# Cross-attention and feed-forward block: early rows of maxima split, transposed and sent ahead of norms, constants and key transfers

## The chip, the core and the metric

One core of one Trainium2 chip runs the kernel. The metric is the device time of one execution in microseconds; the median of several runs is given, with their lowest and highest. Some times below come from one execution that the hardware profiler recorded.

## The reference, cut to what matters

```python
def layer(x, ctx, pos):                 # x (4,256,256), ctx (4,256,128), float32
    h = layernorm(x)
    q = rope(h @ Wq)                    # 32 heads of 8
    k, v = rope((ctx @ Wkv)[k half]), (ctx @ Wkv)[v half]
    w = softmax(q k^T / sqrt(8))        # over 256 keys
    x = x + (w @ v) @ Wout + bout
    h = layernorm(x)
    up = square(relu(h @ up_w)) @ down_w            # 256 -> 1024 -> 256
    moe = (h @ expert_weight) * sum(top2(h @ gate_w))
    return x + layernorm(up + moe) * gamma + beta
```

## The kernel before

The work is cut into 8 tiles of 128 tokens (two for each of 4 batches). Attention is done in 32 rows, numbered M: four rows for each tile of queries, and a row holds 8 heads. Each row goes through these steps:

- **Scores once, for the maxima.** Four units `S(M, i)` of matmuls of queries by keys, each into one PSUM bank of 128x512. VectorE reduces each unit to its negated maxima (`rd.M.i`, line 744, the tile mneg), and so frees the bank.
- **Split.** GpSimd splits the maxima into a high and a low part (`mh.M`, lines 536 and 537, the tile mnat).
- **Transpose.** TensorE transposes them (`MT.M`, the helper at line 817), ScalarE copies the result to mT (`aMT.M`, line 556), and SyncE sends it by DMA into spare rows of qstack (`sM.M`, line 465). Thus the second product has the maximum subtracted in it.
- **Scores again, transposed.** Four units `ST(M, i)` (line 856); ScalarE takes the exponential (`ex.M.i`, line 627). `PV.M` (line 940) multiplies by the values, and the rest is the output projection and the feed-forward part.

A burst `B.a.b@banks` issues two units ST (for a over 0) and two units S (for b over 0) together. Beside that stand, for each batch b, `cT.b` and `K.b` (context and keys), `xT.b` and `Q.b` (normed tokens transposed, query product), VectorE's `dK` and `dQ` (two products each by cosine and sine, lines 732 and 733), the turn by `pad` (lines 350 and 351, on GpSimd for most), `hi` and `lo` (the halves of the value, ScalarE line 615, VectorE or GpSimd line 358), and `sc`, the DMAs that put these into kstack and qstack (line 377). `nm1.b` is the norm of a batch (line 409), and `stackq.i` a memset of a qstack (line 491).

The order of the work is written out by hand in five tables, one for each engine: PE_ORDER, DVE_ORDER, ACT_ORDER, POOL_ORDER and SP_ORDER. Each engine runs its table strictly in order and waits by semaphores. The digits behind @ in PE_ORDER name the PSUM banks of the units. A unit that takes a bank waits until the unit that had it before is emptied, by the engine that reads it. With 8 banks, this ties the order of one engine to that of the others: an entry waits at the head of its engine's table, and all that stands behind it waits too.

Transposes are matmuls with the identity; a float32 matmul appears twice in the trace. Row M may be sent only while the mT buffer M mod 2 is free, and mneg has 3 buffers.

Of the kernel before, what the change touches and what calls it, by code (L numbers as in the profile page):

```python
# [5 lines left out]

PE_ORDER = """
id.7 cT.0@0 id.8 TR.0@1 K.0@2 id.2 xT.0.0@3 id.14 xT.0.1@4 Q.0.0@5 Q.0.1@6 V.0@0 cT.1@1 TR.1@3 id.4 K.1@2 V.1@4
TR.2@5 TR.3@6 cT.2@0 id.23 B.0.1@13 B.0.2@72 xT.1.0@1 B.0.3@42 B.0.4@67 B.0.5@13 B.0.6@54 Q.1.0@0 MT.0@6
B.0.7@12 B.0.8@76 xT.2.0@5 MT.1@4 K.2@2 B.1.9@6541 Q.2.0@0 B.2.10@5617 B.3.0@43 xT.3.0@5 MT.2@0 B.0.11@16 PV.0@0  # L10
MT.3@7 B.4.12@6307 Q.3.0@5 MT.4@2 B.5.13@4160 PV.1@3 B.6.14@7254 B.7.15@0136 MT.5@5 B.8.16@2405 MT.6@3 PV.2@1
B.9.17@7524 PV.3@0 B.10.18@6137 B.11.19@4520 o.0@1 MT.7@7 PV.4@6 B.12.20@2534 B.13.21@0671 MT.8@2 aT.0@3 PV.5@5
B.14.22@4310 B.15.23@2756 W.0@4 MT.9@1 MT.10@3 B.16.24@0267 PV.6@4 B.17.25@1350 B.18.26@6274 PV.7@1 B.19.27@0256
# [14 lines left out]
"""  # L28
DVE_ORDER = """
ang bn1.0.0 bn1.0.1 nm1.0.0 dK.k.0 nm1.0.1 pad.k.0 lo.k.0 dQ.q.0.0 dQ.q.0.1 bn1.1.0 bn1.2.0 lo.q.0.0 dK.k.1  # L30
bn1.3.0 lo.q.0.1 pad.k.1 rd.0.2 rd.0.1 rd.0.0 rd.0.3 rd.1.2 rd.1.0 rd.2.2 rd.1.3 rd.1.1 rd.2.0 rd.2.1 rd.3.3
# [987 lines left out]
```

How the kernel before makes its waits and increments, by code:

```python
        def filled(eng, e):  # L310
            eng.wait_ge(bg_full, FULL[e])
# [4 lines left out]
        def taken(eng, e):  # L317
            eng.wait_ge(bank_free[BANK[e]], TURN[e] + 1)
# [15 lines left out]
        def sent_before(eng, w, b):  # L335
            if b >= 1 and w == "k":
                eng.wait_ge(k_sent[b - 1], 96)
            elif b >= 1:
                for p in range(len(tokens_of(b - 1))):
                    eng.wait_ge(q_sent[b - 1, p], 96)
# [1 line left out]
        def turn_pairs(eng, e):  # L343
            w, b, n = e[1], e[2], cols(e)
            taken(eng, ("K", b) if w == "k" else ("Q", b, e[3]))
            for before in jobs_before(e):
                eng.wait_ge(lo_ready[before], 1)
            r, c, d = rotated[w], by_cos[w], by_sin[w]
            ins = eng.tensor_tensor(r[:, 0, n], c[:, 0, n], d[:, 1, n], ALU.subtract)
            ins = eng.tensor_tensor(r[:, 1, n], c[:, 1, n], d[:, 0, n], ALU.add)
            ins.then_inc(rotated_ready[job(e)], 1)
# [1 line left out]
        def low_part(eng, e):  # L354
            w, b, n = e[1], e[2], cols(e)
            eng.wait_ge(hi_ready[job(e)], 1)
            sent_before(eng, w, b)
            eng.tensor_tensor(lo[w][:, :, n], rotated[w][:, :, n], hi[w][:, :, n].bitcast(f32), ALU.subtract)\
                .then_inc(lo_ready[job(e)], 1)
# [1 line left out]
        def to_stack(eng, e, waited):  # L361
# [8 lines left out]
            if (e[1:-1], high) not in waited:  # L370
                waited.add((e[1:-1], high))
                eng.wait_ge((hi_ready if high else lo_ready)[job(e[:-1])], 1)
                eng.wait_ge(const[at], 1)
```

## Time and profile before

| | us |
|---|---|
| median of 3 runs | 213.78 |
| lowest and highest | 211.82, 215.93 |
| profiled execution | 210.77 |
| its span in the trace | 209.0 |
| TensorE busy in the span | 190.0 |
| VectorE, ScalarE, GpSimd busy | 142.8, 120.5, 84.5 |

The span runs from the first to the last instruction of the trace, the time of the profiled execution includes 1.77 us around it. Busy time counts pipelined matmuls as the profile models their ends, so a busy TensorE need not be at its peak. A row of the timeline gives its start, its length, the engine and line, what it writes and reads with the count, and in brackets how long the engine had been idle before and who released it.

### The profile page before, as it was taken

What the parts mean: (1) busy time and instruction counts of PE and PEld (TensorE: products, weight loads), DVE (VectorE), ACT (ScalarE), POOL (GpSimd) and SP (SyncE); (2) the same over time, 40 slices, a digit from 0 to 9 for tenths busy, and PEclk for the clock granted to TensorE, in tenths of its full rate; (3) what the DMA queues carried; (4) which work ended last, traced back from release to release, by engine and by line L of the source; (5) the groups of instructions that cost most, each with busy time, mean ns of one, the idle gap of its engine ahead of it and who ended that gap; (6) DMA issues with size and microseconds to landing.
All of it is one profiled execution on the core that took longest, in us unless ns stands there. A gap on an engine that the chain in (4) does not pass through costs nothing.

```text
span 209.0 us, 6609 instructions
## 1 busy us (share of the span) xinstructions
PE 190.0 (91%) x2506; PEld 161.0 (77%) x2506; DVE 142.8 (68%) x297; ACT 120.5 (58%) x275; POOL 84.5 (40%) x169
## 2 busy tenths in 40 slices
PE   3989498878899999999999999999999999999990
PEld 2889376656777878888777888778999988999980
DVE  1689497998899888678899986775420558245324
ACT  5743433579788987858676777769572111421400
POOL 6549787982933202410472314121211116263203
PEclk9999958999999999999999999999999999999997
DMA  6919632486544300000042000000000000000001
GB/s 165 313 30 271 130 85 47 107 241 181 168 129 106 108 9 6 3 3 3 5 125 62 5 3 8 5 3 28 5 3 0 28 22 31 0 2 3 25 0 50
DMA packets 15999, 13.15 MB, mean 63 GB/s; under 512 B 2912, under 2 KB 15584, under 8 KB 15968
## 3 DMA queue, kind: packets, MB, share of 16 engines
q1 hardware_dynamic: 11136, 9.32, 15.9%
q10 hardware_dynamic: 4832, 3.42, 6.4%
q8 instruction: 20, 0.33, 0.7%
q14 instruction: 11, 0.09, 0.1%
HBM read 5.13 MB, written 1.05 MB: 30 GB/s over the span
## 4 chain that ended last, share of the span: by engine, by line
PE 66%; DMA 10%; SPq 6%; DVE 4%; issue 4%; POOL 3%; ACT 3%; ACTq 1%; POOLq 0%; DVEq 0%
PE ps L823 24%; PE ps L991 12%; PE ps L940 10%; PE ps L856 9%; PE ps L817 6%; PE ps L846 4%; DMA qstack<-mT 3%; SPq L377 3%; DMA x_sb<-in_x 3%; DMA qstack<-hi_q 2%; ACT probs L627 2%; DMA kstack<-lo_k 1%; SPq L437 1%; ACTq L377 1%; DVE xn L409 1%
## 5 line engine op out<-in xcount | busy, mean ns | idle before, releaser
L744 DVE TENSOR_REDUCE mneg<-ps 128x2 f32<-128x512 f32 x128 | 81.0, 683 | 15.2 <-PE ps L846 15.0
L627 ACT ACTIVATE probs<-ps 128x512 f32<-128x512 f32 x128 | 69.1, 595 | 15.3 <-PE ps L856 13.9
L856 PEld LDWEIGHTS ps<-qstack,kstack 32*128 32x128 f32 x512 | 32.7, 185 | 14.6 <-issue 10.3
L856 PE MATMUL ps<-qstack,kstack 32*128 32x128 f32 x512 | 40.0, 282 | 3.2 <-DMA qstack<-mT 1.5
L940 PE MATMUL ps<-probs,vaug 128*32 128x128 f32 x1024 | 34.0, 275 | 0.6 <-ACT probs L627 0.4
L846 PE MATMUL ps<-kstack,qstack 32*128 32x256 f32 x256 | 32.0, 338 | 2.5 <-DMA qstack<-hi_q 2.1
L823 PE MATMUL ps<-x2nT,up 128*128 128x128 f32 x256 | 31.0, 276 | 0.1
L823 PEld LDWEIGHTS ps<-x2nT,up 128*128 128x128 f32 x256 | 30.2, 192 | 0.7 <-issue 0.2
L991 PE MATMUL ps<-down,inner 128*128 128x256 f32 x128 | 29.5, 379 | 0.0
L940 PEld LDWEIGHTS ps<-probs,vaug 128*32 128x32 f32 x1024 | 26.3, 109 | 3.5 <-issue 1.6
L536 POOL TENSOR_SCALAR mnat<-mneg 128x8 fp32r<-128x8 f32 x32 | 7.6, 236 | 49.2 <-DVE mneg L744 37.8
L991 PEld LDWEIGHTS ps<-down,inner 128*128 128x128 f32 x128 | 23.5, 190 | 2.9 <-issue 0.2
L846 PEld LDWEIGHTS ps<-kstack,qstack 32*128 32x128 f32 x256 | 19.3, 190 | 4.3 <-issue 3.3
L660 ACT ACTIVATE whole<-ps 128x512 f32<-128x512 f32 x16 | 9.6, 602 | 18.0 <-PE ps L823 17.8
L503 POOL TENSOR_SCALAR var_eps<-mv 128x1 f32<-128x1 f32 (+1 forms) x21 | 5.3, 251 | 36.0 <-DVE mv L674 35.8
L548 POOL TENSOR_TENSOR inner<-whole 128x512 f32<-128x512 f32 x9 | 9.4, 1045 | 18.0 <-ACT whole L660 18.0
L504 POOL TENSOR_TENSOR rstd<-var_eps,neg_half 128x1 f32<-128x1 f32 (+1 forms) x21 | 12.9, 613 | 1.7
L788 DVE TENSOR_TENSOR y<-ps,moe 128x256 f32<-128x256 f32 x8 | 3.4, 422 | 14.5 <-PE ps L991 14.5
L556 ACT ACTIVATE oT<-ps 128x128 f32<-128x128 f32 x32 | 8.9, 279 | 6.6 <-PE ps L940 6.3
L883 PE MATMUL ps<-ident 128*128 128x128 f32 x58 | 9.0, 312 | 3.4 <-POOL ident L488 3.4
L556 ACT ACTIVATE mT<-ps 16x128 fp32r<-16x128 f32 x32 | 8.1, 258 | 6.7 <-PE ps L817 5.3
L883 PEld LDWEIGHTS ps<-ident 128*128 128x128 f32 x58 | 7.9, 163 | 3.5 <-POOL ident L488 3.4
(95 smaller groups left out, 251.9 us busy)
## 6 DMA issues: line engine op xcount, KB each, us to landing
kstack<-hi_k SPq DMA_DIRECT2D x12, 128.0 KB, 2.6
qstack<-hi_q SPq DMA_DIRECT2D x11, 128.0 KB, 3.1
kstack<-lo_k SPq DMA_DIRECT2D x8, 128.0 KB, 2.5
result<-x_sb SPq DMA_DIRECT2D x8, 128.0 KB, 1.7
down<-in_L_ffn_down_w ACTq DMA_DIRECT2D x3, 256.0 KB, 4.1
qstack<-lo_q SPq DMA_DIRECT2D x5, 128.0 KB, 2.6
x_sb<-in_x SPq DMA_DIRECT2D x2, 256.0 KB, 5.1
up<-in_L_ffn_up_w SPq DMA_DIRECT2D x1, 512.0 KB, 6.6
```

Source lines behind the costliest of these rows:

```text
L504: pool.tensor_tensor(rstd[:, i, a:z], var_eps[:, i, a:z], neg_half[:, 0:z - a], ALU.pow)\
L556: emptied(act.activation(to, of, ACT.Copy), e)
L627: act.activation(probs[M % NPROBS][:, i, :, :, :], bg(("ST", M, i))[:].rearrange("p (s t n) -> p s t n", s=2, t=T), ACT.Exp, scale=SCALE). ...
L660: emptied(act.activation(whole[j][:], bg((f"up{j}", u))[:].rearrange("p (f n) -> p f n", f=4), ACT.Relu), (f"up{j}", u))
L744: emptied(dve.tensor_reduce(mneg[M % NNEG][:, i, :], bg(("S", M, i))[:].rearrange("p (s k) -> p s k", s=2), AX.X, ALU.max, negate=True), ( ...
L817: ins = pe.transpose(bg(e)[0:rows, at:at + P], block_, ident[:])
L823: ins = pe.matmul(to, lhs[k], rhs[k], start=(k == 0), stop=(k == len(lhs) - 1))
L846: return pe.matmul(bg(("S", M, i))[:, s * N:(s + 1) * N], qstack[b][strip(i), 2 * m + s, tile(t)], kstack[b % 2][strip(i), 2 * m + s, :], ...
L856: return pe.matmul(bg(("ST", M, i))[:, at:at + P], kstack[b % 2][strip(i), 2 * m + s, tile(k)], qstack[b][strip(i), 2 * m + s, tile(t)], s ...
L883: pe.transpose(ps[WARM][:, 0:P], ident[:], ident[:])
L940: ins = pe.matmul(bg(e)[strip(i), 0:P], vaug[b % 2][:, k, NM * i + m, 2 * HD * s:2 * HD * s + Q], probs[M % NPROBS][:, i, s, k, :], start= ...
L991: ins = pe.matmul(bg(("dn", u))[:, 0:D], inner[u % 2][:, f, :], down[:, f, :], start=(f == 0), stop=(f == FT - 1))
```

## The change

The tables alone are edited; the instructions and the banks of each entry stay the same. In PE_ORDER MT.0 goes ahead of B.0.6 and Q.1.0, MT.1 ahead of xT.2.0, MT.2 and B.2.10 ahead of Q.2.0, and K.2 behind B.3.0. DVE_ORDER has the reductions of rows 1 to 4 in another order. ACT_ORDER has aMT.0 ahead of the key DMAs, aMT.1 ahead of axT.2.0, aMT.2 ahead of ex.0.3 and hi.q.1.0. POOL_ORDER has mh.0 ahead of nm1.2.0, and the memsets stackq.2 and stackq.3 behind mh.3 and mh.4. SP_ORDER has sM.0 ahead of the key transfers and sM.2 ahead of the query transfers of batch 1.

```diff
 PE_ORDER = """
...
-TR.2@5 TR.3@6 cT.2@0 id.23 B.0.1@13 B.0.2@72 xT.1.0@1 B.0.3@42 B.0.4@67 B.0.5@13 B.0.6@54 Q.1.0@0 MT.0@6
-B.0.7@12 B.0.8@76 xT.2.0@5 MT.1@4 K.2@2 B.1.9@6541 Q.2.0@0 B.2.10@5617 B.3.0@43 xT.3.0@5 MT.2@0 B.0.11@16 PV.0@0
+TR.2@5 TR.3@6 cT.2@0 id.23 B.0.1@13 B.0.2@72 xT.1.0@1 B.0.3@42 B.0.4@67 B.0.5@13 MT.0@6 B.0.6@54 Q.1.0@0
+B.0.7@12 B.0.8@76 MT.1@4 xT.2.0@5 B.1.9@6541 B.2.10@5617 MT.2@0 Q.2.0@0 B.3.0@43 K.2@2 xT.3.0@5 B.0.11@16 PV.0@0
...
 DVE_ORDER = """
...
-bn1.3.0 lo.q.0.1 pad.k.1 rd.0.2 rd.0.1 rd.0.0 rd.0.3 rd.1.2 rd.1.0 rd.2.2 rd.1.3 rd.1.1 rd.2.0 rd.2.1 rd.3.3
-rd.3.1 rd.3.2 dQ.q.1.0 rd.4.3 rd.3.0 rd.4.2 rd.2.3 dQ.q.2.0 rd.4.0 lo.q.1.0 rd.4.1 rd.5.3 dK.k.2 rd.5.2 rd.5.0
+bn1.3.0 lo.q.0.1 pad.k.1 rd.0.2 rd.0.1 rd.0.0 rd.0.3 rd.1.0 rd.1.2 rd.2.2 rd.1.3 rd.1.1 rd.2.1 rd.2.0 rd.3.1
+rd.3.2 rd.2.3 dQ.q.1.0 rd.3.3 rd.4.3 rd.3.0 rd.4.2 dQ.q.2.0 rd.4.0 lo.q.1.0 rd.4.1 rd.5.3 dK.k.2 rd.5.2 rd.5.0
...
 POOL_ORDER = """
...
-rs1.3.0 nm1.2.0 mh.0 stackq.2 mh.1 lo.k.1 nm1.3.0 pad.q.1.0 stackq.3 mh.2 mh.3 pad.q.2.0 mh.4 pad.k.2 mh.5
+rs1.3.0 mh.0 nm1.2.0 mh.1 lo.k.1 nm1.3.0 mh.2 pad.q.1.0 mh.3 stackq.2 mh.4 stackq.3 pad.q.2.0 pad.k.2 mh.5
...
```

On TensorE, around the query product of batch 2, this stood before (L856 are units ST, L846 units S, L817 transposes, L823 products; mnat are the maxima, Q.b reads xnT and wq_rows, K.b reads cT and wk_rows):

```order
L823 MATMUL ps<-cT,wk_rows 128x256 x2
L856 MATMUL ps<-qstack,kstack 128x128 x2
L846 MATMUL ps<-kstack,qstack 128x256 x2
L856 MATMUL ps<-qstack,kstack 128x128 x4
L846 MATMUL ps<-kstack,qstack 128x256 x2
L856 MATMUL ps<-qstack,kstack 128x128 x2
L823 MATMUL ps<-xnT,wq_rows 128x256 x4
```

The same place now:

```order
L846 MATMUL ps<-kstack,qstack 128x256 x2
L856 MATMUL ps<-qstack,kstack 128x128 x4
L846 MATMUL ps<-kstack,qstack 128x256 x2
L856 MATMUL ps<-qstack,kstack 128x128 x4
L846 MATMUL ps<-kstack,qstack 128x256 x2
L856 MATMUL ps<-qstack,kstack 128x128 x2
L817 MATMUL ps<-ident,mnat 16x128
L823 MATMUL ps<-xnT,wq_rows 128x256 x4
L856 MATMUL ps<-qstack,kstack 128x128 x8
L823 MATMUL ps<-cT,wk_rows 128x256 x2
```

Between the bursts B.1.9 and B.2.10 no product stands any more: the query product (Q.2.0) has moved behind the second burst and behind the transpose of the maxima of row 2, and the key product behind B.3.0.

On ScalarE, the same stretch before (mT0 and mT1 are the two buffers of transposed maxima, probs the exponentials, ps0 is PSUM bank 0):

```order
L556 ACTIVATE mT0<-ps6 16x128
L556 ACTIVATE xnT<-ps5 128x512
L556 ACTIVATE mT1<-ps4 16x128
L627 ACTIVATE probs0<-ps5 128x512
L627 ACTIVATE probs0<-ps6 128x512
L615 ACTIVATE hi_q<-rotated_q 128x512
L627 ACTIVATE probs0<-ps5 128x512
```

and now:

```order
L556 ACTIVATE mT0<-ps6 16x128
L377 DMA kstack1<-hi_k 16x8x256 x2
L556 ACTIVATE mT1<-ps4 16x128
L556 ACTIVATE xnT<-ps5 128x512
L627 ACTIVATE probs0<-ps5 128x512
L627 ACTIVATE probs0<-ps6 128x512
L627 ACTIVATE probs0<-ps5 128x512
L556 ACTIVATE mT0<-ps0 16x128
```

The copy of row 2's maxima out of bank 0 (the last row) now stands behind the third exponential and ahead of the fourth; before, it stood behind the fourth and the query work.

On GpSimd, before (mnat is the split of the maxima, the MEMSETs fill qstack2 and qstack3):

```order
L350 TENSOR_TENSOR rotated_q<-by_cos_q,by_sin_q 128x256
L351 TENSOR_TENSOR rotated_q<-by_cos_q,by_sin_q 128x256
L491 MEMSET qstack3 128x2048
L536 TENSOR_SCALAR mnat0<-mneg2 128x4x2
L537 TENSOR_TENSOR mnat0<-mneg2,mnat0 128x4x2
L536 TENSOR_SCALAR mnat1<-mneg0 128x4x2
L537 TENSOR_TENSOR mnat1<-mneg0,mnat1 128x4x2
```

and now:

```order
L491 MEMSET qstack2 128x2048
L536 TENSOR_SCALAR mnat0<-mneg1 128x4x2
L537 TENSOR_TENSOR mnat0<-mneg1,mnat0 128x4x2
L491 MEMSET qstack3 128x2048
L350 TENSOR_TENSOR rotated_q<-by_cos_q,by_sin_q 128x256
L351 TENSOR_TENSOR rotated_q<-by_cos_q,by_sin_q 128x256
L350 TENSOR_TENSOR rotated_k<-by_cos_k,by_sin_k 128x256
```

Both memsets come later: qstack3's now stands behind the split of row 4 and ahead of the query turn of batch 2 and the key turn.

## Rows read from the trace of the kernel before

**Rows 1.** The page: busy time, share and instructions by engine

```profile
PE 190.0 (91%) x2506; PEld 161.0 (77%) x2506; DVE 142.8 (68%) x297; ACT 120.5 (58%) x275; POOL 84.5 (40%) x169
```

**Rows 2.** Stretches: length, busy PE, PEld, DVE, ACT, POOL (count), clock, DMA share, GB/s

```profile
20.00:35.00 15.00, 11.99 (x74) 9.09 (x72) 10.21 (x21) 5.25 (x12) 11.48 (x15) 0.77 0.44 101
35.00:50.00 15.00, 12.37 (x174) 9.25 (x172) 14.00 (x24) 9.89 (x23) 11.11 (x18) 1.00 0.58 158
50.00:65.00 15.00, 13.27 (x280) 10.59 (x283) 13.99 (x25) 12.91 (x33) 8.30 (x16) 1.00 0.55 157
65.00:100.00 35.00, 34.19 (x656) 28.42 (x645) 28.36 (x51) 28.94 (x69) 7.82 (x26) 1.00 0.11 28
...
22.14:25.57 3.43, 0.52 (x8) 0.34 (x8) 0.79 (x2) 2.16 (x5) 2.73 (x4) 1.00 0.51 117
25.57:32.40 6.83, 6.75 (x28) 5.08 (x29) 5.97 (x10) 1.88 (x4) 5.27 (x8) 0.50 0.33 77
35.50:40.00 4.50, 3.56 (x42) 2.85 (x41) 4.50 (x9) 2.57 (x5) 4.50 (x5) 1.00 0.23 62
```

**Rows 3.** TensorE's timeline from 24 to 49 us

```profile
24.27 0.52 PE L846 MATMUL ps<-kstack,qstack 32*128 32x256 f32 x8 [2.13 <-DMA qstack<-hi_q]
...
29.02 3.65 PE L823 MATMUL ps<-xnT,wq_rows 128*128 128x256 f32 x8
...
32.70 1.02 PE L846 MATMUL ps<-kstack,qstack 32*128 32x256 f32 x8
...
35.25 0.33 PE L856 MATMUL ps<-qstack,kstack 32*128 32x128 f32 x2
...
36.50 1.97 PE L823 MATMUL ps<-xnT,wq_rows 128*128 128x256 f32 x8 [0.57 <-DVE by_sin_q L733]
38.40 0.33 PE L856 MATMUL ps<-qstack,kstack 32*128 32x128 f32 x2
...
40.57 0.28 PE L817 MATMUL ps<-ident,mnat 128*16 128x128 f32 x1
...
48.30 0.33 PE L856 MATMUL ps<-qstack,kstack 32*128 32x128 f32 x2
```

**Rows 4.** VectorE's timeline from 27 to 39 us

```profile
27.46 4.28 DVE L744 TENSOR_REDUCE mneg<-ps 128x2 f32<-128x512 f32 x7 [0.20 <-PE ps L846]
33.27 1.89 DVE L744 TENSOR_REDUCE mneg<-ps 128x2 f32<-128x512 f32 x3 [1.53 <-PE ps L846]
...
38.67 0.68 DVE L732 TENSOR_TENSOR by_cos_q<-ps,table 128x512 f32<-128x512 f32 x1
```

**Rows 5.** The chain that ended last: start, us, what

```profile
40.31 0.22 POOL mnat L537
...
47.94 4.65 DMA qstack<-mT
...
59.20 2.47 DMA qstack<-mT
```

**Rows 6.** GpSimd's timeline from 26 to 44 us

```profile
26.88 2.44 POOL L409 TENSOR_SCALAR xn<-x_sb,mv,rstd 128x256 f32<-128x256 f32 x2 [1.93 <-PE ps L817]
...
38.25 1.81 POOL L491 MEMSET qstack<- 128x2048 f32 x1
40.03 0.20 POOL L536 TENSOR_SCALAR mnat<-mneg 128x8 fp32r<-128x8 f32 x1
...
43.62 0.72 POOL L350 TENSOR_TENSOR rotated_k<-by_cos_k,by_sin_k 128x256 f32<-128x256 f32 x1 [0.30 <-DVE by_sin_k L733]
```

**Rows 7.** ScalarE's timeline from 39 to 47 us

```profile
39.09 0.60 ACT L627 ACTIVATE probs<-ps 128x512 f32<-128x512 f32 x1
...
45.06 0.63 ACT L615 ACTIVATE hi_k<-rotated_k 128x512 fp32r<-128x512 f32 x1
46.59 0.27 ACT L556 ACTIVATE mT<-ps 16x128 fp32r<-16x128 f32 x1 [0.90 <-DMA qstack<-mT]
```

**Rows 8.** TensorE's waits from 46 to 112 us: total, times, longest

```profile
PE ps L856 <- DMA qstack<-mT: 1.5, 3, 0.9
```

More of the change, by code:

```diff
@@ L48 @@
 sc.k.0.0 aV.0 acT.1 aTR.1 hi.q.0.0 ldup.1 sc.q.0.0.0 sc.q.0.0.3 sc.q.0.0.2 hi.q.0.1 sc.q.0.0.1 sc.q.0.1.0
-sc.q.0.1.3 exptab aV.1 aTR.3 axT.1.0 aTR.2 hi.k.1 acT.2 sc.k.1.1 sc.k.1.3 aMT.0 axT.2.0 aMT.1 ex.0.1 ex.0.0
-hi.q.1.0 ex.0.2 sc.q.1.0.3 ex.0.3 lddown.0 aMT.2 sc.q.1.0.5 ex.1.1 aPV.0 aMT.3 axT.3.0 ex.1.0 ex.1.2 ex.1.3
+sc.q.0.1.3 exptab aV.1 aTR.3 axT.1.0 aTR.2 hi.k.1 acT.2 aMT.0 sc.k.1.1 sc.k.1.3 aMT.1 axT.2.0 ex.0.1 ex.0.0
+ex.0.2 aMT.2 ex.0.3 hi.q.1.0 sc.q.1.0.3 lddown.0 sc.q.1.0.5 ex.1.1 aPV.0 aMT.3 axT.3.0 ex.1.0 ex.1.2 ex.1.3
 lddown.2 ldvec.0 hi.k.2 aMT.4 ex.2.0 ex.2.1 aPV.1 hi.q.2.0 ex.2.3 ex.3.0 aMT.5 ex.3.1 ex.2.2 ex.3.2 ex.3.3
@@ L77 @@
 ldwkv ldx.0.0 ldx.2.0 ldx.1.0 ldx.0.1 ldc.2 ldup.0 ldc.1 sc.k.0.2 sc.k.0.3 sc.k.0.5 ldvec.1 sc.k.0.4 sc.q.0.0.4
-sc.q.0.0.5 sc.q.0.1.2 sc.q.0.1.1 sc.q.0.1.5 sc.q.0.1.4 sc.k.1.2 sc.k.1.0 sM.0 ldexpert.1 sc.k.1.4 sM.1 sc.k.1.5
-sc.q.1.0.1 sc.q.1.0.2 sc.q.1.0.0 sM.2 ldexpert.0 sc.q.1.0.4 sM.3 ldwout ldc.3 sM.4 lddown.1 sc.q.2.0.1
+sc.q.0.0.5 sc.q.0.1.2 sc.q.0.1.1 sc.q.0.1.5 sc.q.0.1.4 sM.0 sc.k.1.2 sc.k.1.0 sM.1 ldexpert.1 sc.k.1.4 sc.k.1.5
+sM.2 sc.q.1.0.1 sc.q.1.0.2 sc.q.1.0.0 ldexpert.0 sc.q.1.0.4 sM.3 ldwout ldc.3 sM.4 lddown.1 sc.q.2.0.1
 sc.q.2.0.3 sM.5 sc.q.2.0.0 sc.q.2.0.5 sc.q.2.0.2 sc.q.2.0.4 sM.6 sc.q.3.0.1 sc.q.3.0.3 sM.7 sc.q.3.0.0
```

## The prediction

> **What bounds the kernel now.** I read the totals first: TensorE is busy 190.0 of 209.0 us [rows 1], so the end moves only if TensorE's idle time or its clock moves. The stages say where that can be [rows 2]. From 65 to 100 us TensorE is busy 34.19 of 35 us and VectorE only 28.36: what arrives late at 65 us stays late. Between 35 and 65 us it is VectorE that is full (14.00 and 13.99 of 15) while TensorE has 2.63 and 1.73 us idle. From 20 to 35 us both wait, and the granted clock averages 0.77. The change lies in the last two of these, so I followed 24 to 50 us engine by engine.
>
> I use the names of the order tables. B.0.3 is a burst of matmuls, MT.M the transpose of the maxima of row M, Q.b the query product of batch b, rd a reduction by VectorE, dQ its two products, ex an exponential.
>
> TensorE [rows 3]: two bursts at 24.27, then Q.1.0 from 29.02 for 3.65 us at half clock (the same product took 1.97 us at full clock, Q.2.0 at 36.50). Only behind it stand MT.0 and B.0.7, B.0.8 (32.70). B.1.9, the first burst that uses maxima, starts at 35.25, and B.2.10 at 38.40. MT.2 comes at 40.57. VectorE [rows 4] does seven reductions in 4.28 us, so one each (4.28 - 0.68)/6 = 0.60 us; it waits 1.53 us for the burst behind Q.1.0, starts again at 33.27, and takes Q.2.0's result at 38.67. The chain of waits [rows 5] runs over a memset of GpSimd (38.25 in [rows 6]), the maxima at 40.31, and a transfer of maxima sent at 47.94 that took 4.65 us behind larger ones (another took 2.47).
>
> **Part 1: MT.0 goes ahead of B.0.6 and Q.1.0.** rd.0.3 ends at 27.26. GpSimd, which now does the split before the norm, takes about 0.5 us for the two steps (row 2's began at 40.03 [rows 6] and ended at 40.31 + 0.22 = 40.53 [rows 5]), so maxima are ready at 27.8. MT.0 also needs bank 6, so rd.1.0, which now stands before rd.1.2. It can begin when B.0.4 is full, some 0.15 us after the 27.46 at which the reductions went on before: 27.61 to 28.29. MT.0 runs at 28.3, and the copy by ScalarE behind cT's ends near 29.05. SyncE sends it at 29.1, where before MT.0 itself had to wait for the end of Q.1.0 at 32.5. Past it go two key transfers on either queue, about 0.65 us later each; keys of batch 1 are not read before batch 1's first burst, beyond 50 us, so that costs nothing. rd.1.2, which B.0.6 waits for, is one reduction (0.60) and those 0.15 us later, so B.0.6 and Q.1.0 behind it are 0.75 late: Q.1.0 starts at 29.77, with the clock back near 32.4, and B.0.7 and B.0.8 run together at 32.93, the latter no longer waiting for mT. VectorE now asks first for a bank of B.0.8 (rd.3.1), which is full at 33.45. It restarts at 33.50, before 33.27. So this part, which sends maxima 4 us earlier, leaves VectorE 0.23 us later. The norm of batch 2 moves from 26.88 to 27.8, takes 2.44 us [rows 6] and ends at 30.2, well before its transposes at 33.5: hidden.
>
> **Part 2: rd.2.3 ahead, MT.2 ahead of Q.2.0.** VectorE: rd.3.1 at 33.50, rd.3.2, rd.2.3, dQ.1.0 (35.30 to 36.50: two instructions of 0.68 us as the reductions, so 0.60 apart, 1.20), rd.3.3, rd.4.3, rd.3.0 (37.70 to 38.38), rd.4.2 to 38.98. B.1.9 needs rd.3.2 alone and starts at 34.9, 0.35 earlier. B.2.10 needs rd.3.0, so 38.50, 0.1 later. Before, Q.2.0 filled the time between these two bursts (36.50 to 38.40) and VectorE took its result at once, at 38.67. Now Q.2.0 stands behind MT.2, in the same bank 0, and behind B.2.10. So it must wait for B.2.10 (38.5), MT.2 (39.0), and the copy aMT.2, which on ScalarE stands behind ex.0.2, an exponential of B.2.10 that took 0.60 us and began 0.69 after it (39.09 in [rows 7]): 39.2 to 39.8, copy to 40.0. Q.2.0 starts at 40.05, needs 1.97 us at full clock and is there at 42.02. VectorE's next instruction after rd.4.2 is dQ.2.0: **it waits from 38.98 to 42.07**, against 38.67 before: +3.4 us on the engine that is full in this stage. The gain on the other side: mT.2 leaves at 40.0, earlier than before, where MT.2 was only transposed at 40.57, and ahead of the large query transfers; the 0.90 us that ScalarE waited for it at 46.59 [rows 7] goes.
>
> **Part 3: two memsets of GpSimd go behind the splits.** Each takes 1.81 us [rows 6]. They no longer delay MT.2. But the split of row 4 must wait for rd.4.1, now at 45.14 (dQ.2.0 43.26, rd.4.0, lo, rd.4.1), and behind it stand a memset (1.8), the query turn (1.4) and the key turn (0.72 twice): 45.65 + 1.8 + 1.4 + 1.45 = 50.3. In before the key turn started at 43.62. ScalarE has hi_k next in its order, at 45.06 before [rows 7], now at 50.35, and behind it the copy of MT.4 (51.1) and ex.2.0 (done 51.7). B.6.14 needs both: 51.75 instead of 48.30 [rows 3], +3.45 us. That is the lag leaving the changed region at full clock.
>
> **The clock.** In before the granted clock was 1.00 until 25.57, though TensorE had been busy only 0.52 of the 3.43 us ahead of it, and was 0.50 for the next 6.83 us, in which it was busy 6.75 [rows 2]. The new order makes such a stretch again: B.1.9 ends near 35.6, then nothing until 38.5, then B.2.10 (0.6) and MT.2 (0.3), nothing until 40.05. That is 0.9 busy of 4.5 us, where before had 3.56 of 4.5 and kept 1.00 [rows 2]. I expect a second fall near 39 us. All of Q.2.0 would then run at half: 3.65 - 1.97 = 1.7 more, so the bounds of this term are 0 and 1.7, and something more if K.2 and PV.0 run slow too, which VectorE's five instructions after Q.2.0 (3 us) partly hide. I take 1.7, since the earlier low stretch lasted 6.8 us although TensorE was full.
>
> The Trainium skill ("TensorE: Matmul & The Clock Gate", Part 4: PE-mode transpose) states that transposes do not count as busy for the clock in the way matmuls do. By that rule MT.2 would hold nothing up and the fall would be surer; the sum would be the same. No row here separates the two kinds. On transfers "DMA: Bandwidth & Descriptors" (Queues, rings and completion order) says that a transfer's completion write lands only after every earlier write of that DMA engine. By that rule sending small maxima ahead of large transfers gives back up to 4.65 - 2.47 = 2.2 us per transfer; the trace agrees that they differ so, and the saving would speak for the change (the third case below).
>
> **What comes back.** TensorE's waits after 46 us for transfers of maxima are 1.5 us in three [rows 8], of which 0.86 lies before B.6.14 and is counted already; 0.6 is left, which a late kernel hides. The idle of VectorE (1.01) and TensorE (1.73) between 50 and 65 us bounds what the stretch can take back. With a small lag I take 1.2, with a large one 1.7.
>
> **The sum.** Against the profiled execution (210.77 us, span 209.0): 3.45 + 1.7 - 1.7 = +3.4, so 214.2. The three runs have a median of 213.78, 3.0 above it; the difference carries over: 217.2.
>
> **Rivals.**
> 1. The replay holds but the clock doesn't fall again: 3.45 - 1.2 = +2.2, 216.0. For it: a burst of 0.6 us lies in the middle of the gap. Against: [rows 2], the fall at 25.57. Chance 0.2.
> 2. Faster: maxima are the bound, as the chain [rows 5] says. Then MT.2 at 39.0 instead of 40.57 gives 1.5, and the waits for transfers 0.6 more: -2.1, 211.7. It decides if VectorE's wait for Q.2.0 is made up by the work that piles up behind it before 65 us. Against: VectorE has only 1.0 us idle in 15. Chance 0.15.
> 3. The order has slack that cancels, the stall is shorter than computed, say 0.6 us: no change, 213.8. Chance 0.12.
> 4. No catching up, and K.2, xT.3.0 and PV.0 slow as well: 3.45 + 1.7 + 0.5 = +5.6, 219.4. Chance 0.1.
>
> The main case has the remaining 0.43. A measurement of this kernel can tell about 2% from no change, here 4.28 us. Slower by more than that: rival 4 and a quarter to a third of the main case, 0.24. Faster by more than 2%: a third of rival 2, 0.05. Within: 0.71. The range reaches from near rival 2, 212.5, to beyond rival 4, 220.5.
>
> **What would show it.** Right: B.0.7 near 32.9 and VectorE going on at 33.5; no matmul between about 35.6 and 38.5; Q.2.0 starting near 40.05 behind a copy of mT; a gap of VectorE before by_cos_q of 3 to 5 us; a granted clock of 0.5 from about 39; the key turn past 50 us; more idle of TensorE in the stage from 35 to 50, and an unchanged stage after 80 us. Wrong: Q.2.0 before 39, a VectorE gap under 1 us there, or a TensorE that is back on the old times by 65 us.

## Result and profile after

The changed kernel takes 219.55 us (median of 4 runs, 218.26 to 220.34), the kernel before 213.53 us (median of its 4): slower, ratio 1.030 with a 95% interval of 1.021 to 1.039. The profiled execution took 218.26 us, span 216.5 against 209.0.

Each run also reports the mean clock that TensorE was granted, and this number matters here: the same kernel runs at different clocks from run to run. In seven of the twelve profiled executions of the experiments (e2, e3, e4, e6, e7, e9, e11) it was at least 0.01 below the kernel's median; from those I read waits, their causes and the course of the clock, never a total. Ratios compare only runs that were not disturbed (within 1.5% of their kernel's fastest), each with the runs of before made beside it, while medians are over all runs.

The page of the changed kernel: span, busy time by engine, TensorE's busy tenths and the granted clock in 40 slices.

```profile
span 216.5 us, 6609 instructions
...
PE 194.3 (90%) x2506; PEld 164.2 (76%) x2506; DVE 142.2 (66%) x297; ACT 120.5 (56%) x275; POOL 84.0 (39%) x169
...
PE   3999395699888999999999999999999999999990
...
PEclk9999958558999999999999999999999999999997
```

TensorE is busy 4.3 us longer for the same 2506 matmuls, and the clock row has a second low stretch two slices after the first. The stages, to be read beside [rows 2]:

```profile
20.00:35.00 15.00, 10.62 (x67) 7.81 (x65) 9.11 (x18) 5.30 (x12) 9.25 (x13) 0.77 0.41 93
35.00:50.00 15.00, 11.03 (x65) 8.16 (x69) 8.09 (x14) 3.66 (x8) 7.92 (x12) 0.55 0.40 108
50.00:65.00 15.00, 12.82 (x252) 9.93 (x245) 13.16 (x23) 11.94 (x28) 10.54 (x17) 1.00 0.55 143
65.00:100.00 35.00, 33.42 (x611) 27.44 (x603) 29.47 (x55) 29.20 (x71) 9.26 (x28) 1.00 0.20 54
33.08:36.49 3.41, 2.12 (x27) 1.31 (x25) 2.46 (x5) 1.25 (x3) 1.77 (x2) 1.00 0.06 7
36.49:50.14 13.65, 10.51 (x57) 7.78 (x61) 6.74 (x13) 3.03 (x7) 6.57 (x11) 0.50 0.42 118
```

From 35 to 50 us VectorE is busy 8.09 us instead of 14.00, and the clock is 0.55 instead of 1.00. Where VectorE was full, it now waits. The last two lines show the clock's fall: in the 3.41 us before it TensorE was busy 2.12, and in the low stretch it was busy 10.51 of 13.65 us. In before, the stretch behind the first low stretch looked like this, and no fall followed:

```profile
32.40:35.82 3.42, 3.40 (x31) 2.35 (x29) 2.55 (x5) 1.01 (x3) 2.25 (x3) 1.00 0.11 18
```

TensorE's timeline, for [rows 3]:

```profile
24.40 0.51 PE L846 MATMUL ps<-kstack,qstack 32*128 32x256 f32 x8 [2.62 <-DMA qstack<-hi_q]
...
29.89 3.55 PE L823 MATMUL ps<-xnT,wq_rows 128*128 128x256 f32 x8
33.37 0.52 PE L846 MATMUL ps<-kstack,qstack 32*128 32x256 f32 x8
...
35.37 0.33 PE L856 MATMUL ps<-qstack,kstack 32*128 32x128 f32 x2 [0.83 <-DVE mneg L744]
...
39.05 0.47 PE L856 MATMUL ps<-qstack,kstack 32*128 32x128 f32 x2 [3.02 <-DVE mneg L744]
...
41.05 3.75 PE L823 MATMUL ps<-xnT,wq_rows 128*128 128x256 f32 x8 [0.58 <-ACT mT L556]
...
45.78 2.07 PE L823 MATMUL ps<-cT,wk_rows 128*128 128x256 f32 x4
...
49.36 1.43 PE L940 MATMUL ps<-probs,vaug 128*32 128x128 f32 x32
...
55.74 0.33 PE L856 MATMUL ps<-qstack,kstack 32*128 32x128 f32 x2
```

Q.1.0 starts at 29.89 and B.0.7 at 33.37. B.1.9 runs at 35.37, then B.2.10 comes after 3.02 us of idle. Q.2.0 starts at 41.05 (36.50 before) and takes 3.75 us, K.2 (45.78) takes 2.07 where it took 1.03, and PV.0 starts at 49.36 where it started at 41.36. B.6.14 starts at 55.74, 7.4 us late. VectorE, for [rows 4]:

```profile
27.73 4.27 DVE L744 TENSOR_REDUCE mneg<-ps 128x2 f32<-128x512 f32 x7 [0.35 <-PE ps L846]
34.03 1.89 DVE L744 TENSOR_REDUCE mneg<-ps 128x2 f32<-128x512 f32 x3 [2.02 <-PE ps L846]
...
44.84 0.69 DVE L732 TENSOR_TENSOR by_cos_q<-ps,table 128x512 f32<-128x512 f32 x1 [5.34 <-PE ps L823]
...
49.50 0.69 DVE L744 TENSOR_REDUCE mneg<-ps 128x2 f32<-128x512 f32 x1 [1.57 <-PE ps L846]
```

The wait ahead of by_cos_q is 5.34 us, against none in before. There is another of 1.57 us at 49.50, for B.0.11 behind the slow K.2 and xT.3.0. GpSimd and ScalarE, for [rows 6, 7]:

```profile
39.42 1.81 POOL L491 MEMSET qstack<- 128x2048 f32 x1
48.02 0.20 POOL L536 TENSOR_SCALAR mnat<-mneg 128x8 fp32r<-128x8 f32 x1 [6.80 <-DVE mneg L744]
...
48.45 1.81 POOL L491 MEMSET qstack<- 128x2048 f32 x1
...
51.59 0.72 POOL L350 TENSOR_TENSOR rotated_k<-by_cos_k,by_sin_k 128x256 f32<-128x256 f32 x1
```

```profile
53.21 0.63 ACT L615 ACTIVATE hi_k<-rotated_k 128x512 fp32r<-128x512 f32 x1
```

Row 4's split waits 6.80 us, then come the memset, the query turn and the key turn (51.59), and hi_k is at 53.21 instead of 45.06.

The lateness is then carried to the end almost without change. PV.3, PV.4 and PV.6 begin 8.0, 7.8 and 8.0 us later than in before, a PV row near 97 us 8.0, and the last PV row, at 173.8 us in before, 7.5. The span is 7.5 longer.

### The profile page after: what moved, and what is told of

Its sections match the earlier page's. It is cut to its first block, busy times and chain, and to the rows that moved or that the text cites. A ratio compares the mean times of both kernels' runs of the same rounds, so it can differ in the third digit from the quotient of the medians.

```text
span 216.5 us, 6609 instructions
## 1 busy us (share of the span) xinstructions
PE 194.3 (90%) x2506; PEld 164.2 (76%) x2506; DVE 142.2 (66%) x297; ACT 120.5 (56%) x275; POOL 84.0 (39%) x169
## 3 DMA queue, kind: packets, MB, share of 16 engines
q10 hardware_dynamic: 4832, 3.42, 6.0%
HBM read 5.13 MB, written 1.05 MB: 29 GB/s over the span
## 4 chain that ended last, share of the span: by engine, by line
PE 71%; DVE 9%; DMA 5%; issue 5%; ACT 3%; POOL 2%; SPq 2%; ACTq 1%; POOLq 0%; DVEq 0%
PE ps L823 28%; PE ps L991 12%; PE ps L940 10%; PE ps L856 10%; PE ps L817 6%; DVE mneg L744 5%; PE ps L846 4%; DMA qstack<-hi_q 2%; DMA qstack<-lo_q 2%; PE ps L883 2%; SPq L377 2%; ACT probs L627 1%; DMA qstack<-mT 1%; ACTq L377 1%; POOL qstack L491 1%
## 5 line engine op out<-in xcount | busy, mean ns | idle before, releaser
L856 PEld LDWEIGHTS ps<-qstack,kstack 32*128 32x128 f32 x512 | 33.5, 189 | 19.3 <-issue 13.1
L856 PE MATMUL ps<-qstack,kstack 32*128 32x128 f32 x512 | 41.1, 286 | 7.4 <-DVE mneg L744 4.1
L846 PE MATMUL ps<-kstack,qstack 32*128 32x256 f32 x256 | 32.4, 342 | 2.8 <-DMA qstack<-hi_q 2.6
L823 PE MATMUL ps<-x2nT,up 128*128 128x128 f32 x256 | 31.0, 276 | 0.0
L823 PEld LDWEIGHTS ps<-x2nT,up 128*128 128x128 f32 x256 | 30.2, 192 | 0.7
L536 POOL TENSOR_SCALAR mnat<-mneg 128x8 fp32r<-128x8 f32 x32 | 7.1, 221 | 59.3 <-DVE mneg L744 47.9
L846 PEld LDWEIGHTS ps<-kstack,qstack 32*128 32x128 f32 x256 | 19.8, 194 | 4.4 <-issue 4.3
L823 PE MATMUL ps<-xnT,wq_rows 128*128 128x256 f32 (+1 forms) x40 | 11.2, 443 | 0.6 <-ACT mT L556 0.6
```

The source lines that it names most:

```text
L823: ins = pe.matmul(to, lhs[k], rhs[k], start=(k == 0), stop=(k == len(lhs) - 1))
L846: return pe.matmul(bg(("S", M, i))[:, s * N:(s + 1) * N], qstack[b][strip(i), 2 * m + s, tile(t)], kstack[b % 2][strip(i), 2 * m + s, :], ...
L856: return pe.matmul(bg(("ST", M, i))[:, at:at + P], kstack[b % 2][strip(i), 2 * m + s, tile(k)], qstack[b][strip(i), 2 * m + s, tile(t)], s ...
```

## Experiments

Clocks differ between runs, so I give for each kernel its median, the ratio with its interval, the median of the runs' mean clocks, and the span reduced to full clock: over the 54 runs of before the span grows by 0.39 us for each microsecond spent at half clock (2 x (1 - clock) x span), and that much is taken off each run's span. The reduced span in the table is the mean over a kernel's runs. These scatter by 0.4 to 1.5 us (standard deviation), so that a mean over 4 runs is good to 0.2 to 0.8 us; and the reduction is rough where another kernel's low stretches lie in other places. For the changed kernel it runs from 207.5 to 210.7.

| kernel | median us | ratio to before, 95% | median clock | reduced span |
|---|---|---|---|---|
| before (54 runs) | 214.05 | 1 | 0.959 | 205.6 |
| changed | 219.55 | 1.030 (1.021 to 1.039) | 0.948 | 209.0 |
| e1 changed, idle matmuls in the gap | 218.79 | 1.013 (0.992 to 1.034) | 0.958 | 209.3 |
| e2 changed, Q.2.0 ahead again | 216.17 | 1.012 (0.997 to 1.028) | 0.968 | 208.7 |
| e3 changed, Q.2.0 ahead of MT.2 | 222.08 | 1.031 (1.016 to 1.046) | 0.942 | 210.0 |
| e4 before, 41 warming transposes | 212.25 | 0.996 (0.990 to 1.001) | 0.972 | 206.6 |
| e5 before with part 1 alone | 214.94 | 1.012 (0.977 to 1.047) | 0.952 | 205.8 |
| e6 before, Q.2.0 behind B.2.10 | 213.90 | 1.013 (0.995 to 1.031) | 0.963 | 206.3 |
| e7 as e1, memset moved | 216.00 | 1.015 (0.984 to 1.047) | 0.967 | 208.9 |
| e8 as e2, memset moved | 216.73 | 1.021 (0.983 to 1.059) | 0.966 | 208.5 |
| e9 changed, row 2's part undone | 215.92 | 1.015 (1.003 to 1.026) | 0.956 | 206.6 |
| e10 changed, part 1 undone | 217.58 | 1.024 (1.015 to 1.034) | 0.948 | 207.0 |
| e11 before, idle matmuls ahead | 212.03 | 0.999 (0.994 to 1.004) | 0.978 | 207.1 |
| e12 before, idle matmuls in bursts | 214.11 | 1.003 (0.997 to 1.009) | 0.976 | 208.0 |

My theory was the order (VectorE waits for Q.2.0), made worse by the clock. Rivals: GpSimd's key turn behind a memset, and the early row 0.

**e1: does the clock double the loss?**

```diff
-B.1.9@6541 B.2.10@5617 MT.2@0 Q.2.0@0
+B.1.9@6541 fl.7 B.2.10@5617 MT.2@0 fl.1 Q.2.0@0
+                elif what == "fl":
+                    begin(("ST", 1, 1))
+                    for _ in range(e[1]):
+                        pe.matmul(ps[3][:, 0:N], ident[:], wkv[:, 0:N], start=True, stop=True)
```

> The changed kernel with idle filler on TensorE: seven matmuls (identity by 256 columns of a weight) into the empty bank 3 ahead of B.2.10, one more behind MT.2. They compute nothing that is used. Theory order plus clock: the stall behind Q.2.0 stays, but the clock is at full for Q.2.0, K.2 and PV.0. Then Q.2.0 takes 2.0 us instead of 3.75, PV.0 begins 3 to 4 us earlier than in the changed kernel, and the time falls by 3 to 4, to about 216 us. Rival, order alone (the low clock is hidden by VectorE): time stays within 1 us of 219.5. Rival, the key turn on GpSimd sets the end: also no gain.

In the profiled execution the span is 212.6 at clock 0.978, the same clock as before's profiled 209.0: 3.6 us of the 7.5 are left, so in this pair of executions 3.9 hung on the clock. The idle matmuls, the burst, Q.2.0, PV.0 and B.6.14:

```profile
35.66 3.29 PE L884 MATMUL ps<-wkv,ident 128*128 128x256 f32 x14
38.88 0.33 PE L856 MATMUL ps<-qstack,kstack 32*128 32x128 f32 x2
...
40.47 1.97 PE L823 MATMUL ps<-xnT,wq_rows 128*128 128x256 f32 x8 [0.28 <-ACT mT L556]
...
44.88 1.08 PE L944 MATMUL ps<-probs,vaug 128*32 128x128 f32 x32
...
52.07 0.33 PE L856 MATMUL ps<-qstack,kstack 32*128 32x128 f32 x2 [1.09 <-ACT probs L627]
```

```profile
32.70:36.11 3.41, 2.57 (x29) 1.75 (x29) 2.39 (x4) 1.18 (x3) 1.70 (x2) 1.00 0.05 7
36.11:50.00 13.89, 13.10 (x127) 10.02 (x129) 10.39 (x19) 5.37 (x13) 8.87 (x15) 1.00 0.50 141
```

```profile
50.66 0.63 ACT L615 ACTIVATE hi_k<-rotated_k 128x512 fp32r<-128x512 f32 x1 [2.21 <-POOL rotated_k L351]
```

The clock stays at 1.00, Q.2.0 takes 1.97 us, and PV.0 begins at 44.88 instead of 49.36. In this run order alone acts, and it acts nearly as the replay said: B.6.14 was to start at 51.75 and starts at 52.07, hi_k was to be at 50.35 and is at 50.66. But the median was to come to 216 and is 218.79: the other three runs had lower mean clocks (0.964, 0.952, 0.938; where they fell is not on record). The reduced span, 209.3, doesn't differ from the changed kernel's 209.0. So the price of the clock rests on one execution of either kernel; in the medians it is not shown.

**e2: one entry put back.**

```diff
-B.2.10@5617 MT.2@0 Q.2.0@0
+Q.2.0@0 B.2.10@5617 MT.2@0
```

> The changed kernel with one entry put back: Q.2.0 ahead of B.2.10, as before. Theory order plus clock: VectorE has Q.2.0 in time, the gap of TensorE is filled, no second fall of the clock; PV.0 back near 41.5 to 42 us, time 213 to 214.5, that is nearly all of the 6 us. Rival, the key turn on GpSimd (the two memsets behind the splits): it still starts past 46 us, and the time stays 2 to 3 us above before.

A miss: 216.17 us, and PV.0 was still late (45.98). One cause is the clock, which fell again, at 37.91, before Q.2.0 began (38.38), and was back at 41.32. ScalarE shows the other, in the copy of row 2's maxima, ex.0.3 and hi_q:

```profile
43.63 0.27 ACT L556 ACTIVATE mT<-ps 16x128 fp32r<-16x128 f32 x1 [0.62 <-PE ps L817]
43.80 0.57 ACT L627 ACTIVATE probs<-ps 128x512 f32<-128x512 f32 x1
44.28 0.61 ACT L615 ACTIVATE hi_q<-rotated_q 128x512 fp32r<-128x512 f32 x1
```

MT.2 must wait until VectorE has emptied Q.2.0's bank, and ScalarE's order has its copy ahead of ex.0.3 and hi_q. The query (rotated_q) had been ready since 40.1 and ScalarE free since 43.0; VectorE then waits another 1.21 us for hi_q, ahead of lo_q. The entry put back moved part of the stall to another engine: Q.2.0, MT.2 and the copy are tied through one bank, and one of them alone can't be undone.

**e3: is it the shared bank?**

```diff
-B.2.10@5617 MT.2@0 Q.2.0@0
+B.2.10@5617 Q.2.0@0 MT.2@0
```

> The changed kernel with Q.2.0 ahead of MT.2, still behind B.2.10. The wait for the copy of row 2's maxima (0.6 us idle and the transpose, together 1 us) is gone, the gap of 3 us between the two bursts stays. Theory order plus clock: 1 to 1.5 us faster than the changed kernel, clock still falls, 218 us. Rival, the shared bank is the main cost: as fast as with Q.2.0 wholly ahead, 214 us.

1 to 1.5 us of gain were expected, and none came: ratio 1.031, as the changed kernel. The transpose of the maxima now waits:

```profile
45.63 0.37 PE L817 MATMUL ps<-ident,mnat 128*16 128x128 f32 x1 [1.47 <-DVE by_sin_q L733]
```

It stands at 45.63 instead of 40.09, and the copy behind it holds ScalarE back as in e2. VectorE's wait ahead of by_cos_q is 4.41 us instead of 5.34, and then it waits 1.31 us for hi_q. So what the wait for the copy cost comes back on the other side.

**e9: row 2's part put back on TensorE, ScalarE and SyncE.** VectorE's and GpSimd's orders stay as changed, and so do part 1, MT.1, xT.2.0 and K.2.

```diff
-B.2.10@5617 MT.2@0 Q.2.0@0 B.3.0@43 K.2@2 xT.3.0@5 B.0.11@16
+Q.2.0@0 B.2.10@5617 B.3.0@43 K.2@2 xT.3.0@5 MT.2@0 B.0.11@16
-ex.0.2 aMT.2 ex.0.3 hi.q.1.0 sc.q.1.0.3 lddown.0 sc.q.1.0.5
+hi.q.1.0 ex.0.2 sc.q.1.0.3 ex.0.3 lddown.0 aMT.2 sc.q.1.0.5
-sM.2 sc.q.1.0.1 sc.q.1.0.2 sc.q.1.0.0 ldexpert.0
+sc.q.1.0.1 sc.q.1.0.2 sc.q.1.0.0 sM.2 ldexpert.0
```

> The changed kernel with all of row 2's part put back on the three engines that it touches: Q.2.0 ahead of B.2.10, MT.2 behind xT.3.0, its copy behind ex.0.3 and hi_q, its transfer behind the query transfers. Putting Q.2.0 back alone had left the copy of row 2 ahead of ex.0.3 and hi_q, so that these two waited for it (ex.0.3 at 43.8, hi_q at 44.3 us). Theory: the loss sits in the ring Q.2.0, MT.2, copy, ex.0.3, hi_q, and all of it goes: 213.5 to 214.5, at equal clock within 1 us of before. Rival, GpSimd's memsets and splits keep 2 to 3 us: 216.

The median falls by 3.6 us to 215.92, the reduced span from 209.0 to 206.6: 2.4 of the 3.4 us that the order costs. What stays is 1.0 us at equal clock, as the theory had it; the median itself came out at the rival's 216 (ratio 1.015, 1.003 to 1.026). Its trace names two remnants:

```profile
38.86 3.36 PE L823 MATMUL ps<-xnT,wq_rows 128*128 128x256 f32 x8 [1.22 <-DVE by_sin_q L733]
...
51.83 0.33 PE L856 MATMUL ps<-qstack,kstack 32*128 32x128 f32 x2 [0.58 <-ACT probs L627]
```

Q.2.0 waits 1.22 us for VectorE, 0.65 more than in before: rd.2.3, one reduction, still stands ahead of dQ.1.0. It takes 3.36, since the clock had fallen at 38.27 in this run too, although Q.2.0 stood ahead of B.2.10 again; K.2 was still behind B.3.0. And B.6.14 waits 0.58 us for exponentials that stand behind hi_k on ScalarE. The stretch ahead of the fall, and the low one:

```profile
34.86:38.27 3.41, 1.95 (x26) 1.31 (x25) 2.64 (x5) 1.43 (x4) 1.95 (x2) 1.00 0.06 7
38.27:41.68 3.41, 2.82 (x7) 2.31 (x8) 2.83 (x5) 1.15 (x3) 3.21 (x8) 0.50 0.28 77
```

**e10: part 1 undone, and e5: part 1 alone.** In e10 the entries of row 0 (MT.0, rd.1.0, mh.0, aMT.0, sM.0) go back to their old places in the changed kernel; in e5 they alone are moved in before:

```diff
-B.0.5@13 B.0.6@54 Q.1.0@0 MT.0@6
+B.0.5@13 MT.0@6 B.0.6@54 Q.1.0@0
-rd.0.3 rd.1.2 rd.1.0
+rd.0.3 rd.1.0 rd.1.2
-acT.2 sc.k.1.1 sc.k.1.3 aMT.0
+acT.2 aMT.0 sc.k.1.1 sc.k.1.3
-rs1.3.0 nm1.2.0 mh.0
+rs1.3.0 mh.0 nm1.2.0
-sc.k.1.2 sc.k.1.0 sM.0
+sM.0 sc.k.1.2 sc.k.1.0
```

> The changed kernel without part 1 (MT.0 and its split, copy and transfer back at their places of before; rows 1 and 2 as changed). Theory: row 2's part carries the loss, so it stays: gap of VectorE ahead of by_cos_q 3.3 to 5 us, 218 to 219.5. Rival, the early row 0 is what hurts: 214 to 215.

> The kernel before with part 1 alone: MT.0 ahead of B.0.6 and Q.1.0, rd.1.0 ahead of rd.1.2, and the split, copy and transfer of row 0 ahead of the norm and of the key transfers. By my replay Q.1.0 starts 0.75 us later, B.0.8 no longer waits for the copy, and VectorE restarts 0.2 us later or at the same time: 0 to +0.6 us, 213.5 to 214.5. Rival, early maxima are worth something: 1 us faster.

Without part 1 the kernel stays slower (ratio 1.024), and VectorE's wait for Q.2.0 is the same 5.34 us:

```profile
44.38 0.69 DVE L732 TENSOR_TENSOR by_cos_q<-ps,table 128x512 f32<-128x512 f32 x1 [5.34 <-PE ps L823]
```

Alone, part 1 gives no gain; its cost can't be told from nothing (reduced span +0.2, ratio 1.012 with a wide interval). Early maxima of row 0 bought nothing that the runs show: in the changed kernel the first burst that uses them waited 0.83 us for a bank that VectorE had to empty. How much part 1 costs inside the changed kernel stays open. The reduced spans of e10 and the changed kernel differ by 2.0 us, e5's from before's by 0.2, and the two profiled executions at the same clock (0.947) by 1.0, with by_cos_q 0.46 us earlier in e10.

**e6: Q.2.0 behind B.2.10, nothing else.**

```diff
-B.1.9@6541 Q.2.0@0 B.2.10@5617
+B.1.9@6541 B.2.10@5617 Q.2.0@0
```

> The kernel before with one entry moved: Q.2.0 behind B.2.10. MT.2 stays where it was. Theory order: B.2.10 runs at 37.7 and Q.2.0 at 38.3 instead of 36.5, so VectorE waits for it until 40.3 instead of 38.7: 1.6 us slower, 215 us, without a second fall of the clock, since the gap is under 2 us. If the clock falls too, 2.5 to 3.5 us slower. Rival, the place of Q.2.0 costs nothing by itself: 213.5.

```profile
42.67 0.69 DVE L732 TENSOR_TENSOR by_cos_q<-ps,table 128x512 f32<-128x512 f32 x1 [1.57 <-PE ps L823]
```

VectorE waits 1.57 us where 1.6 was expected. The kernel is 0.7 us slower by reduced span, ratio 1.013 (0.995 to 1.031), so about half of this wait reaches the end, as far as four runs can tell. The stall in the changed kernel is 3.27 us at full clock (e1). Against the 1.57 of e6, MT.2 and its copy between burst and product account for 1.0: in e6 Q.2.0 follows the burst at once, in e1 it comes 0.9 us behind its end. The other 0.7 is for the most part the burst itself. VectorE's new order has rd.3.0, which B.2.10 waits for, third of the four reductions ahead of dQ.2.0, where it was second; so the burst starts 0.3 us before the four are done in e1 (0.5 in the changed kernel), and 1.05 in e6.

The clock did not fall in e6 between 35.93 and 56.41 us, though TensorE waited 1.77 us ahead of B.2.10 and Q.2.0 stood behind it. K.2 stood in its old place there:

```profile
35.93:39.35 3.42, 2.35 (x23) 1.73 (x21) 3.42 (x7) 1.75 (x4) 2.51 (x3) 1.00 0.21 48
39.35:42.77 3.42, 2.72 (x24) 2.19 (x24) 1.85 (x4) 1.79 (x4) 3.34 (x5) 1.00 0.20 50
```

**e7 and e8: the memset on GpSimd.**

```diff
-mh.3 stackq.2 mh.4 stackq.3 pad.q.2.0
+mh.3 stackq.2 stackq.3 mh.4 pad.q.2.0
```

> The changed kernel with the filler, and in GpSimd's order the memset of qstack3 directly behind that of qstack2, ahead of row 4's split (GpSimd was idle there for 4.7 us in the run with the filler alone). Theory key turn: hi_k, at 50.7 with the filler alone, starts 1.8 us earlier, the 1.1 us that B.6.14 waited for an exponential go, and the span at equal clock is 1 to 1.3 us shorter than the 212.6 with the filler alone. Rival, the memset is hidden: no difference.

> The changed kernel with Q.2.0 back ahead of B.2.10 and the memset of qstack3 ahead of row 4's split. If the residual 2 us of the run with Q.2.0 ahead (at equal clock) were the key turn behind the memset, this comes to within 1 us of before, 213.5 to 214.5. If they were part 1's lateness and MT.2's wait for Q.2.0 to be emptied, it stays at 215 to 216.

In e7 the wait of 1.1 us ahead of B.6.14 is gone, but the reduced span falls by only 0.4 us (209.3 to 208.9) where 1 to 1.3 were expected, and in e8 by 0.2 (208.7 to 208.5). So the key turn is hardly the main cause; both differences lie within the scatter.

**e4, e11, e12: can the clock be held in the kernel before?**

```diff
-id.23
+id.41
```

```diff
-id.23 B.0.1@13 B.0.2@72 xT.1.0@1
+id.23 fl.0.5 B.0.1@13 B.0.2@72 fl.1.1 xT.1.0@1
```

```diff
                     banks_of_burst(units)
+                    if units[0][0] == "ST" and units[0][2] == 0 and 2 <= units[0][1] <= 7:
+                        for _ in range(2 if units[0][1] == 2 else 1):
+                            pe.matmul(bg(units[2])[:, 0:N], ident[:], wkv[:, 0:N], start=True, stop=True)
```

> The kernel before with 41 warming transposes of the identity instead of 23 ahead of the first burst, so that TensorE is busy through its 2.1 us wait for the query transfer. If transposes hold the clock, it stays at full past 25.6 us, Q.1.0 takes 2.0 instead of 3.65 us, and the kernel is 1 to 2 us faster, about 212 us. If they don't count, the clock falls as before and the time is the same, 213.5 us.

> The kernel before with five idle matmuls (identity by 256 columns of a weight) behind the warming transposes, into the empty bank 7 during the wait for the query transfer, and one more into bank 4 during the 0.8 us behind B.0.2. Theory, matmuls in the wait hold the clock: no fall near 25.6 us, Q.1.0 takes 2.0 instead of 3.65 us, and the kernel is 1 to 2.5 us faster than before, 211.5. Rival: the fall comes anyway or VectorE hides it, 213.5.

> The kernel before with idle matmuls in six bursts, those that wait for the maxima of rows 2 to 7 (two for row 2, one for each other, 0.43 us each at full clock, into the bank that the burst is about to fill). In the traces so far the clock of before-like kernels also fell between 51 and 56 us for 10 to 14 us in several runs, and the spans at clock 0.95 were 4 us above those at 0.98. Theory, light bursts with waits let the clock fall: fewer runs with a mean clock of 0.96 or less, their share down from about half of the runs of before, median 1 to 2 us lower, the best runs 0.5 to 1 us longer than before's best. Rival, these falls don't hang on TensorE's work: same mix of clocks, and 0.5 to 1 us slower throughout.

In their profiled executions e4 and e11 did not do what they were built for: the transfer landed later than in before (first burst at 25.84 and 25.53 instead of 24.27), TensorE still waited 2.02 and 1.47 us for it, the clock fell at 27.13 and 27.88, and Q.1.0 took 3.63 and 3.78 us. So whether transposes hold the clock is not answered. By their mean clocks, 1 of e4's 10 runs and 3 of e11's 12 had no early fall (0.992 to 0.996; before's 54 never passed 0.98), but the spans at 0.992 and 0.996 are 209.0 and 208.4 us, as the best of before at 0.98 (207.6 to 209.8). So Q.1.0's slowness seems to cost little, which would fit a TensorE that waits for VectorE there, and neither kernel is clearly faster: 0.996 (0.990 to 1.001) and 0.999 (0.994 to 1.004). In e12 the mix of clocks does change: 1 of 12 runs has a mean clock of 0.96 or less, where 32 of before's 54 have (11 of the 17 made beside it). The idle matmuls cost 1 to 2.5 us (best span 210.2 against 209.3 beside it, reduced span 208.0 against 205.6), so the sum is the same, 1.003, and the 1 to 2 us of gain that were expected did not come. No version beats the kernel before.

## Why the prediction came out as it did

217.2 us was forecast, in a range of 212.5 to 220.5; 219.55 was measured. The direction, the place and the order term were right. The size was not: +3.4 against +6.0. Two terms failed, the clock's price and what comes back. In the forecast they were +1.7 and -1.7 and cancelled, so its +3.4 is the order term alone; that it still lies within a factor of two of the measured change is partly luck.

**Part 1** came as computed, some 0.1 to 0.3 us later: MT.0 at 28.57 (28.3 forecast), mT sent at 29.27 (29.1), Q.1.0 at 29.89 (29.77). VectorE restarted at 34.03, 0.5 later than the 33.50, since the clock came back at 33.08 in this execution, not at 32.4.

**Part 2's order term** was right. The replay gave 3.45 us at B.6.14 at full clock, and e1 with the clock held shows 52.07 - 48.30 = 3.8. "It waits from 38.98 to 42.07", 3.09 us, is 3.27 us in e1. That this row 2 part carries the larger share of the loss is borne out by e9 (2.4 of 3.4 us go when most of it is put back) and by the wait of 5.34 us that remains in e10; but taking out part 1 also lowers the reduced span, by 2.0 us, so the shares are not settled.

**Part 3** was read rightly as an event (hi_k at 50.66 in e1, 50.35 forecast), and not as a cost: I let it set the lag at B.6.14, and e7 got back 0.4 us, within the scatter.

**The clock.** A second fall came, and a slow Q.2.0 with it. The step that failed is "I expect a second fall near 39 us", with its reason and its price. The clock fell at 36.49, when the long gap had lasted only half a microsecond. The work before the gap had thinned already: K.2, four dense passes of 1.03 us together, had left the stretch from 34.26 on, and TensorE was busy 2.12 of 3.41 us where it had been 3.40 of 3.42. Q.2.0's place was not what made it fall. All six traces in which K.2 stands behind B.3.0, without idle matmuls, have a second fall: at 36.49 (changed), 35.82 (e10) and 38.64 (e3) with Q.2.0 behind B.2.10, and at 37.91 (e2), 38.87 (e8) and 38.27 (e9) with Q.2.0 ahead of it as in before. Those with K.2 in its old place (before, e4, e5, e6, e11) have none up to 51 us, e6 with Q.2.0 behind the burst among them; nor have e1 and e7 with idle matmuls in the gap. (In e12 the first low stretch itself runs to 40.10, so it can't tell.) What Q.2.0's place goes with is the length of the low stretch: 13.65 us with it behind, 3.41 with it ahead. (K.2 alone put back was not tried, and the six share other moves too: MT.1 ahead of xT.2.0 and VectorE's order.) In the changed kernel the clock stayed low for 13.65 us instead of the 6.8 on which the price rested, so that K.2, xT.3.0 and part of PV.0 ran slow too, and VectorE waited a second time. I took 1.7 us for the term; the profiled executions of e1 and of the changed kernel, one of each, differ by 3.9.

The Trainium skill ("TensorE: Matmul & The Clock Gate", What's actually happening) puts it as "the default state is throttled, and activity releases the throttle". No run here shows a default state; that falls followed stretches with little work on TensorE agrees with the traces (0.54 us busy of 3.33 below, 2.12 of 3.41 in the changed kernel). The release does not always come with a busy TensorE: in e4's profiled execution, at a mean clock of 0.951, the clock stayed low through 13.65 us in which TensorE was busy 13.20, the larger part of it with the bursts of lines 846 and 856. Length, busy PE, PEld, DVE, ACT, POOL, clock, DMA share, GB/s of four stretches of e4:

```profile
23.80:27.13 3.33, 0.54 (x9) 0.34 (x8) 0.78 (x2) 0.00 (x0) 0.78 (x2) 1.00 0.09 21
27.13:33.96 6.83, 6.74 (x28) 5.08 (x29) 5.98 (x10) 1.87 (x4) 5.25 (x8) 0.50 0.33 77
49.50:54.40 4.90, 2.98 (x60) 2.03 (x58) 4.50 (x8) 3.80 (x10) 2.45 (x5) 1.00 0.82 228
54.44:68.09 13.65, 13.20 (x180) 10.52 (x184) 7.87 (x14) 7.46 (x19) 5.42 (x10) 0.50 0.36 94
```

**What comes back** failed too. I took 1.7 us off for a large lag; nothing came back between 57 and 109 us, and 0.5 just behind that. So the idle times of [rows 2] and [rows 8] were not slack. I read them as waits in a ring of fixed order (maxima, transfer, exponential, bank) that move along with the lag; no run tests this. Rival 4, "no catching up, and K.2, xT.3.0 and PV.0 slow as well", is what happened; it gave 219.4, and I gave it 0.1. That it meets the median of 219.55 is partly luck: its clock terms are 2.2 us together, where the profiled executions show 3.9.

The sum with measured terms: order 3.4 to 3.6, the clock 3.9 in the profiled execution, nothing back, makes 7.5. In the medians the clock weighs less, because before's runs have falls of their own (median 0.959 against 0.948): 3.4 for the order and (22.6 - 17.4) x 0.39 = 2.0 for the clock are 5.4, of the 5.5 between 219.55 and the 214.05 of before's 54 runs. The 17.4 and 22.6 us at half clock are 2 x (1 - clock) x span of the two medians.

Rival 2, faster by early maxima, found no support: MT.2 did come 0.5 us earlier (40.09 against 40.57), but between 36 and 112 us TensorE still waited 1.2 us for transfers of maxima, against 1.5 in before. The prediction's paragraph on transfers points at this rival as "the third case"; it is the second.

## What to carry to other kernels

Where several engines run fixed orders tied by few banks, replay the instruction that is moved together with everything that now stands behind its wait on every engine; an entry put back alone may leave the stall elsewhere (e2). Don't take idle time downstream as room for catching up unless its releaser would arrive earlier than the lag. And look at what a moved dense product leaves behind on TensorE: here the clock fell in all six traces in which K.2 had left a stretch of short bursts and waits and nothing filled it, and in the one pair of executions that prices it this cost as much as the stall itself (3.9 against 3.6 us).

## What the runs showed of the hardware

The spread between runs of one unchanged kernel goes with the granted clock. Of 54 runs of before, 22 had a mean clock above 0.96 and a median span of 210.05 us, 32 had 0.96 or less and 213.3; the extremes are 207.6 at 0.98 and 224.3 at 0.893. The fit over all is 0.39 us for each microsecond at half clock, and explains 92% of the variance of the spans. In eight traces (e2 to e7, e9, e11) an extra low stretch lies in the stages with many short bursts and waits, between 51 and 76 us, and lasts 7 to 14 us. With idle matmuls ahead of the bursts of rows 2 to 7, runs with a mean clock of 0.96 or less were rarer (e12, 1 of 12). With warming transposes or dense matmuls toward the first transfer a few runs lacked the early fall (e4, 1 of 10, clock 0.992; e11, 3 of 12, up to 0.996), and neither moved the end.
